# Key chunks of the loop as three products of rounded parts, with the context split on GpSimd

## The reference, cut to what matters

```python
q = (layernorm(x) @ w_q.T)         # x: 8 batches, 56 queries, 128 wide; 16 heads of 8
k = (ctx @ w_k.T)                  # ctx: 8 batches, 1500 keys, 128 wide
v = (ctx @ w_v.T)
attn = softmax(q k^T * HEAD_DIM ** -0.5)
x = x + tanh(g_xattn) * (attn v @ w_o.T)
x = x + tanh(g_ffn) * experts(layernorm(x))   # 8 experts, top 2, GELU, F = 512
```

## Time and profile before

| what | value |
|---|---|
| median of 3 runs | 293.86 us (292.49 to 294.77) |
| the profiled execution | 293.01 us, its span 291.3 us |
| granted TensorE clock, mean of the span | 0.994 |
| attention loop with its tail | about 27 to 211 us of the span |

### The profile page before, as it was taken

The page is one execution under the profiler, slowest core; times in us unless marked ns, Lnnn a source line. Parts: engine busy times, 40 slices in busy tenths (PEclk is TensorE's granted clock), DMA queues, the critical chain, the costliest instruction groups (busy, mean ns, idle before and its releaser), DMA issues.

```text
span 291.3 us, 8035 instructions
## 1 busy us (share of the span) xinstructions
PE 279.3 (96%) x2826; PEld 223.8 (77%) x2826; DVE 217.8 (75%) x420; ACT 178.7 (61%) x370; POOL 103.0 (35%) x113
## 2 busy tenths in 40 slices
PE   7988999999999999999999999999899999998994
PEld 2464888878878887887888898987688888887862
DVE  5688878768787687787876877877155988888861
ACT  2635586766766767568568674567517776665500
POOL 4598632052043033224206201024501466676300
PEclk9999799999999999999999999999999999999999
DMA  7397932970991892693397299200000000000001
GB/s 256 96 202 196 223 97 60 263 212 12 248 223 53 214 233 83 164 243 123 96 248 185 52 214 279 101 0 2 2 2 0 1 0 0 0 1 0 2 0 32
DMA packets 9924, 32.19 MB, mean 111 GB/s; under 512 B 2576, under 2 KB 3088, under 8 KB 9904
## 3 DMA queue, kind: packets, MB, share of 16 engines
q1 hardware_dynamic: 9472, 31.60, 42.4%
q10 hardware_dynamic: 432, 0.33, 0.3%
HBM read 13.26 MB, written 0.23 MB: 46 GB/s over the span
## 4 chain that ended last, share of the span: by engine, by line
PE 86%; DVE 5%; ACT 3%; DMA 2%; issue 1%; POOL 1%; SPq 0%; DVEq 0%; ACTq 0%
PE max_ps L963 16%; PE score_ps L943 15%; PE o_ps L977 14%; PE misc_ps L931 8%; PE misc_ps L925 5%; PE score_ps L1185 4%; PE score_ps L1186 3%; PE score_ps L1187 3%; PE o_ps L1267 2%; PE o_ps L1185 1%; ACT probs L514 1%; PE o_ps L1187 1%; PE o_ps L1186 1%; PE max_ps L993 1%; PE misc_ps L1098 1%
## 5 line engine op out<-in xcount | busy, mean ns | idle before, releaser
L700 DVE TENSOR_REDUCE part_max<-max_ps 112x1 f32<-112x512 f32 (+1 forms) x192 | 116.2, 669 | 35.1 <-PE max_ps L963 34.4
L514 ACT ACTIVATE probs<-score_ps 128x448 f32<-128x448 f32 x192 | 90.2, 555 | 13.5 <-PE score_ps L943 12.1
L963 PE MATMUL max_ps<-kx,qx 96*112 96x512 f32 (+1 forms) x192 | 81.1, 428 | 2.0 <-DVE part_max L700 0.9
L943 PE MATMUL score_ps<-qx,kx 104*128 104x224 f32 (+1 forms) x384 | 76.6, 285 | 0.6 <-ACT probs L514 0.4
L943 PEld LDWEIGHTS score_ps<-qx,kx 104*128 104x128 f32 (+1 forms) x384 | 67.0, 190 | 11.2 <-issue 3.2
L977 PE MATMUL o_ps<-probs,v_sb 128*32 128x112 f32 (+1 forms) x1536 | 43.9, 261 | 1.1 <-ACT probs L514 1.1
L977 PEld LDWEIGHTS o_ps<-probs,v_sb 128*32 128x32 f32 (+1 forms) x1536 | 35.7, 110 | 9.1 <-ACT probs L514 6.1
L963 PEld LDWEIGHTS max_ps<-kx,qx 96*112 96x112 f32 x192 | 34.2, 179 | 7.1 <-issue 2.9
L366 POOL TENSOR_TENSOR k_low<-k_full,k_high 128x512 fp32r<-128x512 f32 (+1 forms) x21 | 26.3, 1252 | 33.2 <-ACT k_full L497 32.9
L399 POOL TENSOR_TENSOR o_norm<-o_sb,inv_den 128x112 f32 (+1 forms) x15 | 6.3, 422 | 81.3 <-DVE inv_den L726 81.3
L509 ACT ACTIVATE v_sb<-misc_ps 128x512 f32<-128x512 f32 x24 | 14.4, 600 | 31.2 <-PE misc_ps L931 31.2
(11 more groups left out here) (177 smaller groups left out, 376.2 us busy)
## 6 DMA issues: line engine op xcount, KB each, us to landing
kx<-k_high SPq DMA_DIRECT2D x60, 187.5 KB, 5.1
kx<-k_low SPq DMA_DIRECT2D x30, 187.5 KB, 4.9
ctx_sb<-in_ctxT SPq DMA_DIRECT2D x7, 750.0 KB, 5.8
gu_sb<-in_guT SPq DMA_DIRECT2D x8, 512.0 KB, 5.3
dn_sb<-in_dnT SPq DMA_DIRECT2D x8, 256.0 KB, 5.4
ctx_sb<-in_ctxT SPq DMA_DIRECT2D x2, 256.0 KB, 4.2
kx<-k_high SPq DMA_DIRECT2D x4, 123.5 KB, 2.3
kx<-k_high SPq DMA_DIRECT2D x4, 64.0 KB, 2.0
```

What stands on the lines that cost most here:

```text
L514: nc.scalar.activation(probs[:, (KT * h + t) % 8, :], score_ps[:, t % 3, 0:SC // 2], ACT.Exp, scale=SCALE).then_inc(exp_done, 1)
L700: nc.vector.reduce_max(part_max[:, p, c:c + 1], max_ps[0:PC, bank, 0:size], AX.X).then_inc(max_taken, turns)
L943: last = nc.tensor.matmul(score_ps[0:m, t % 3, GC * g:GC * g + GC], kx[0:KR, 2 * par + h, g, 128 * t:128 * t + m], qx[0:KR, par, 2 * h + g ...
L963: nc.tensor.matmul(max_ps[0:PC, bank, 0:size], qx[0:MR, par, 2 * h + p // 2, PC * (p % 2):PC * (p % 2) + PC], kx[0:MR, slot, p // 2, start ...
```

## The change

The 18 key chunks of the loop are made by three fp32r matmuls (high part of the weights by high part of the context, high by low, low by high) instead of one fp32 matmul. The weights' parts are made once by POOL ahead of the loop. The context's parts are made by POOL for each chunk (`split_context`: an addition of a broadcast zero that writes the rounded part, then a subtraction), into two buffers used in turn, and PE waits for them on `ctx_split`. Two of the first batch's splits stand ahead of `ones_rows(2)`, the third in the first body. SP loads a batch's context in three chunks with a semaphore each. The keys of odd batches take the room of experts 5 to 7 in `gu_sb`, so that these three experts are loaded only after the last odd keys have been moved; POOL's, ACT's and PE's wait for them (`late_loaded`) stands later, in the FFN. POOL's loop has two turns and its last two bodies are written out.

```diff
         def _(sp):
+            def load_chunk(b, par, n):
+                start, size = chunk(n)
+                sp.dma_start(ctx_sb[:, par, start:start + size], ctxT[b][:, start:start + size]).then_inc(chunk_loaded[par][n], 16)
...
                 if ctx_next:
+                    sp.wait_ge(v_done, NCH * (b + 1) + 2)
+                    load_chunk(b + 3, 1 - par, 0)
+                    load_chunk(b + 3, 1 - par, 1)
                     sp.wait_ge(v_done, NCH * (b + 2))
-                    sp.dma_start(ctx_sb[:, 1 - par, 0:TK], ctxT[b + 3]).then_inc(ctx_loaded[1 - par], 16)
+                    load_chunk(b + 3, 1 - par, 2)
...
             pool.wait_ge(consts, 1)
+            nc.gpsimd.memset(no_shift[:, :], 0.0).then_inc(wk_split, 1)
+            pool.wait_ge(wk_split, 1)
+            pool.wait_ge(wk_loaded, 16)
+            nc.gpsimd.tensor_copy(wk_parts[:, 0, :], wk_sb[:, :]).then_inc(wk_split, 1)
+            pool.wait_ge(wk_split, 2)
+            nc.gpsimd.tensor_tensor(wk_parts[:, 1, :], wk_sb[:, :], wk_parts[:, 0, :].bitcast(f32), ALU.subtract
+                                    ).then_inc(wk_split, 1)
+            pool.wait_ge(wk_split, 3)
...
+            def split_context(i, par, n):
+                start, size = chunk(n)
+                side, made = (par + n) % 2, NCH * batch(i, par) + n + 1
+                src = ctx_sb[:, par, start:start + size]
+                pool.wait_ge(chunk_loaded[par][n], 16 * (i + 1))
+                nc.gpsimd.tensor_tensor(ctx_parts[:, side, 0, 0:size], src, bc(no_shift[:, :], [128, size]), ALU.add
+                                        ).then_inc(ctx_high, 1)
+                pool.wait_ge(ctx_high, made)
+                nc.gpsimd.tensor_tensor(ctx_parts[:, side, 1, 0:size], src, ctx_parts[:, side, 0, 0:size].bitcast(f32),
+                                        ALU.subtract).then_inc(ctx_split, 1)
+
             pool.wait_ge(k_low_saved, 2 * NCH)
+            split_context(0, 0, 0)
+            pool.wait_ge(ctx_split, 1)
+            pool.wait_ge(nm_step, 6)
+            split_context(0, 0, 1)
+            pool.wait_ge(ctx_split, 2)
             ones_rows(2)
             ones_rows(3)
...
                 stage(b + 2, par, 0)
+                pool.wait_ge(qx_ready, 2 * b + 5)
+                pool.wait_ge(k_done, NCH * (b + 2) + 1)
+                split_context(i, par, 2)
+                pool.wait_ge(ctx_split, NCH * (b + 1))
                 k_rest(b + 2, par, 1)
                 k_rest(b + 2, par, 2)
                 normalise(i, par, 0)
+                if more:
+                    pool.wait_ge(o_norm_ready, FIRST_NORM + 2 * b + 1)
+                    pool.wait_ge(k_done, NCH * (b + 2) + 2)
+                    split_context(i1, par1, 0)
+                    pool.wait_ge(ctx_split, NCH * (b + 1) + 1)
+                    pool.wait_ge(k_done, NCH * (b + 3))
+                    pool.wait_ge(scores_done, KT * (2 * b + 2) + 1)
+                    split_context(i1, par1, 1)
+                    pool.wait_ge(ctx_split, NCH * (b + 1) + 2)
                 normalise(i, par, 1)
...
+            def k_product(i, par, n):
+                size = chunk(n)[1]
+                pe.wait_ge(ctx_split, NCH * batch(i, par) + n + 1)
+                for k, (w, c) in enumerate(((0, 0), (0, 1), (1, 0))):
+                    last = nc.tensor.matmul(misc_ps[:, 0:size], wk_parts[:, w, :], ctx_parts[:, (par + n) % 2, c, 0:size],
+                                            start=(k == 0), stop=(k == 2), skip_group_check=True)
+                last.then_inc(k_done, 1)
...
                 if h == 0 and c == 0:
-                    pe.wait_ge(ctx_loaded[par], 16 * (i + 2))
                     pe.wait_ge(v_saved, NCH * (b + 1) + 1)
-                    k_project(b + 2, par, 0, misc_ps)
+                    k_product(i, par, 0)
```

More of the change, by code:

```diff
@@ L183, in flamingo_block @@
         k_done, k_saved, k_low_saved = map(sem, ("k_done", "k_saved", "k_low_saved"))
+        wk_split, ctx_high, ctx_split, late_loaded = map(sem, ("wk_split", "ctx_high", "ctx_split", "late_loaded"))
+        chunk_loaded = [[sem(f"chunk_loaded{par}{n}") for n in range(NCH)] for par in range(2)]
         v_done, v_saved = map(sem, ("v_done", "v_saved"))
@@ L245, in move_keys @@
                 eng.dma_start(kx[32 * row:32 * row + 32, 2 * par + h, g, start:start + size].bitcast(f32),
-                              src[r:r + 32, par, start:start + size].bitcast(f32)).then_inc(landed, 16)
+                              src[par][r:r + 32, start:start + size].bitcast(f32)).then_inc(landed, 16)
         @block.sync
         def _(sp):
+            def load_chunk(b, par, n):
+                start, size = chunk(n)
+                sp.dma_start(ctx_sb[:, par, start:start + size], ctxT[b][:, start:start + size]).then_inc(chunk_loaded[par][n], 16)
             def move_unit(par, h):
@@ L270, in _ @@
             sp.wait_ge(v_done, NCH)
-            sp.dma_start(ctx_sb[:, 0, 0:TK], ctxT[2]).then_inc(ctx_loaded[0], 16)
+            for n in range(NCH):
+                load_chunk(2, 0, n)
             sp.wait_ge(k_low_saved, 2 * NCH)
@@ L286, in body, with load_expert @@
                 move_unit(par, 1)
[L287 to L292, removed]
+                if early:
+                    load_expert(b)
+            def load_expert(e, loaded=ffn_loaded):
+                sp.dma_start(gu_sb[:, e, :], guT[:, e, :]).then_inc(loaded, 16)
+                sp.dma_start(dn_sb[:, e, :, :], dnT[:, e, :, :]).then_inc(loaded, 16)
             with sp.Fori(0, 2) as i:
@@ L297, in _ @@
             body(2, 0)
-            body(2, 1, ctx_next=False)
-            for e in range(B - 2, E):
-                load_expert(e)
+            body(2, 1, ctx_next=False, early=False)
+            for h in range(2):
+                for g in range(2):
+                    sp.wait_ge(kx_loaded[2 + h][g], MOVES * B // 2)
+            for e in range(LATE, E):
+                load_expert(e, late_loaded)
             sp.wait_ge(out_ready, NR)
@@ L402, in normalise, with body @@
                                         ).then_inc(o_norm_ready, 1)
-            def body(i, par):
+            def body(i, par, more=True):
                 b = batch(i, par)
+                i1, par1 = nxt(i, par, 1)
                 pool.wait_ge(scores_done, KT * 2 * b + 1)
@@ L413, in body @@
                 normalise(i, par, 0)
+                if more:
[7 more added lines that the diff above has]
+                    pool.wait_ge(ctx_split, NCH * (b + 1) + 2)
                 normalise(i, par, 1)
-            with pool.Fori(0, B // 2 - 1) as i:
+            with pool.Fori(0, 2) as i:
                 body(i, 0)
                 body(i, 1)
+            body(2, 0)
+            body(2, 1, more=False)
             pool.wait_ge(scores_done, KT * (NU - 4) + 1)
@@ L493, in k_copy @@
                 act.wait_ge(k_done, NCH * b + n + 1)
-                nc.scalar.activation(k_high[:, par, start:start + size], bank[:, 0:size], ACT.Copy
+                nc.scalar.activation(k_high[par][:, start:start + size], bank[:, 0:size], ACT.Copy
                                      ).then_inc(k_saved, 1 if whole else 2)
@@ L690, in k_rest @@
                 dve.wait_ge(k_saved, 2 * (NCH * b + n + 1))
-                nc.vector.tensor_tensor(k_low[:, 0, start:start + size], bank[:, 0:size],
-                                        k_high[:, 0, start:start + size].bitcast(f32), ALU.subtract
+                nc.vector.tensor_tensor(k_low[0][:, start:start + size], bank[:, 0:size],
+                                        k_high[0][:, start:start + size].bitcast(f32), ALU.subtract
                                         ).then_inc(k_low_saved, 1)
```

35 lines of the change are left out of this document (22 added, 13 removed).

## The result

| what | before | after |
|---|---|---|
| median, the runs of that measurement | 293.26 us (6 runs) | 296.35 us (295.77 to 297.48, 6 runs) |
| ratio | | 1.0094, 95% interval 1.0056 to 1.0132 |
| profiled execution, its span | 293.01 us, 291.3 us | 297.39 us, 295.6 us |
| granted clock, mean of the span | 0.994 | 0.982 |
| POOL busy | 103.0 us | 145.0 us |

A forecast was written before the change was run, and what follows sets the result against it. PE was taken to bound the loop from end to end. From 293.0 us, 2.5 saved, 3.7 of standing and 1.7 of clock gave 295.9 us profiled, 296.8 us median with 0.85 us added; range 292.6 to 298.8 us.

The forecast's parts named there:

- The stand: First loop body: PE idles 3.7 us from 44.30 us until POOL's third split ends at 48.0; bounds 2.9 to 4.1.
- The rival in which POOL is in time: First body: POOL finishes the third split by 44.0 us, so PE never stands; 291.1 us, chance 0.10.
- The Trainium skill's rule: POOL's splits: two-input operations cost about 2.6 cycles an element, so broadcast saves nothing; PE's idle time 0.3 us longer.
- The clock: PE's clock falls to half rate again around the first body's idle stretch, costing 1.7 us; bounds nothing and 2.5 us.
- The products: Loop's 18 key chunks: three fp32r matmuls save 0.16 us for each of 12, 0.145 for each of 6; 2.8 us.
- a saving of 0.16 us fits into both: Steady loop: PE came 0.35 us behind DVE and 0.39 us behind ACT, so the chunk saving would be kept.
- one of my own signs of being wrong: Steady loop: the prediction is wrong if PE's waits for DVE and ACT at L986 and L977 grow in every unit.
- The rival of a third gone: Loop: DVE and ACT take one third of the saving, beside PE's idle stretch; +1 us, 297.8 us, chance 0.10.
- The 0.08 us that I gave to the change of format: Ahead of a fp32 chunk, the last fp32r matmul takes 0.30 us instead of 0.22; expected to remain behind the product.
- The steady loop: Later bodies: POOL's three splits add 7.1 us per 23.5 us body, all covered by gaps; cost nothing.
- The weights' parts: Ahead of POOL's `q_parts` work: three small POOL instructions may overlap DVE's first block-diagonal operation; 0 to 0.4 us, taken as nothing.
- The sum: Whole kernel: 293.0 - 2.5 + 3.7 + 1.7 = 295.9 us profiled, 296.8 us for the median, 1.0% slower.

The follow-up runs named there:

- The filled stand: Changed kernel with PE's first loop turn written out and 16 unread matmuls of 128 columns ahead of the third chunk's wait: 294.56 us, ratio 1.0040 to the kernel before.
- the control: Changed kernel with only the first turn of PE's loop written out: 297.05 us, ratio 1.0126 to the kernel before.
- fp32 chunks in the same order: Changed kernel with both `ones_rows` memsets ahead of POOL's `nm_step` wait, loop key chunks by one fp32 matmul, POOL's splits kept: 293.21 us, ratio 0.9948.
- free cast, held clock: Changed kernel with `ones_rows(2)` ahead of the `nm_step` wait, `ones_rows(3)` behind the first `normalise`, eight unread matmuls ahead of the loop: 289.75 us, ratio 0.9867.
- the kernel before with the extra matmuls: Kernel before the change with only eight unread matmuls of 128 columns added ahead of the loop: 291.83 us, ratio 0.9941.
- the kernel with one memset moved: Changed kernel with only `ones_rows(2)` moved ahead of POOL's wait for `nm_step`: 292.64 us, ratio 0.9948 to the kernel before.

## Why the prediction came out right

**The stand** is the step that carried it. I had POOL's queue from 34.2 to 48.0 us and a stand of 3.7 us from PE's old time, 4.0 with PE's earlier arrival. Measured: 48.13 and 3.93 us. Each term was near: the additions took 1.04 and 0.98 us (1.06 and 0.99 taken from `stage`), the memsets 5.37, the gap 0.39. The rival in which POOL is in time falls.

The Trainium skill's rule that I set against it (GPSIMD Engine Reference, section 3.1, a `tensor_tensor` of two inputs at about 2.6 cycles an element) would have had the addition at the subtraction's 1.28 us; with a broadcast second input it took 1.04 us. Here the measurement decides against the rule for this form. (By my own bounds the rule would have made the stand 0.4 us longer, not the 0.3 us that stand there.)

**The clock** was put at 1.7 us, between 0 and 2.5. The filled stand says 1.6 us against the changed kernel by the ratios; the profiled execution lost 2.1 us. The 2.5 us to the control hold some of the first fall too. Right in kind, and near in size.

**The products** were mis-sized. I took 2.8 us with 1.8 us as the low end, and let 2.5 us stay. Three measurements say 1.7 us (medians, fp32 chunks in the same order), 1.6 us (18 times the trace's 0.09 us) and 2.1 us (free cast, held clock, the change as a whole). The product's own 0.70 and 0.65 us were right; the step that failed is "a saving of 0.16 us fits into both" gaps behind it. In PE's loop 0.24 us pass from DVE's end to PE's start even when PE waits (0.12 us in the turn written out), so of 0.27 to 0.36 us only 0.03 to 0.12 were free. Half of one of my own signs of being wrong did show: the wait for DVE at L986 grew in every unit of the steady loop, by 0.05 to 0.12 us. The rival of a third gone had the true size. The gap to ACT ahead of `attend` did hold. The 0.08 us that I gave to the change of format are something else, for the last product of the maxima starts 0.31 us ahead of the fp32r chunk too (84.87 to 85.18); what they are stays open. The longer first tile at a turn of the loop was not foreseen and stays unexplained; writing out one turn gained nothing that can be seen.

**The steady loop** at nothing was right: fp32 chunks with all of POOL's new work stay at the kernel before's time. POOL was 42 us busier and not 46; my own 2.4 and 2.3 us a split would have said 43. **The weights' parts** cost nothing either: DVE's operation there, 0.61 us, was not held up.

**The sum** was closer than its terms, and that is luck. Both errors push the same way: a smaller saving and a dearer clock each make the kernel slower than forecast. With the measured terms, 3.9 us for the stand, 1.6 to 2.1 for the clock and 1.7 to 2.1 saved, it should be 3.4 to 4.3 us slower. The profiled execution is, with 4.3 us. The forecast was 2.9 us, and the six runs give 2.8 us, with an interval of 1.6 to 3.9 us and the median between three runs that lost less to the clock and three that lost more.

## What to carry to other kernels

Where a change hangs the busiest engine on another, walk the other's queue through the first turn of the loop as well as a steady one: the work from ahead of the loop lies there, and one wait put in front of it moves all of it. Ask next what the clock does with the new gap: here it added about half of the stand's own time. And a saving is only as large as the slack to the next engine less the time that the hand-over takes, and that time has to be read from a place where the engine really waits; here it was twice as long in PE's loop as in the turn written out.

## What the hardware showed

- A DVE cast of 112 partitions by 4 columns is held up by POOL's memset until that ends: 0.17 us became 0.60, 0.61, 1.59 and 1.60 us in four profiles. POOL's `stage` does it as well: in the kernel before with the extra matmuls the cast took 0.45 us and ended at 33.33, POOL's operation at 33.30. DVE's reductions beside it, the tensor_reduce of 12 columns in SBUF among them (0.17 us), were not touched. The Trainium skill (SBUF — State Buffer, its section on the two separate sides) calls this an exclusive lock of a shared port pair, held for the whole instruction; the trace agrees, with the 1.59 us above. The page says it of DVE operations in a two-port mode; whether the cast ran in one, no trace here shows.
- A split does it to DVE's subtraction of 112 by 4 as well. Inside the stand of the changed kernel it took 0.96 us instead of 0.16 and ended at 46.88, POOL's addition at 46.86. It cost nothing there, since PE stood anyway, and happened nowhere else in that profile.
- From the end of DVE's subtraction to the start of PE's `transpose_max` at least 0.23 us passed in PE's loop, even where PE had stood 1.3 us for it (0.24 us). With the turn written out it was 0.12 to 0.19 us, and at the `transpose_max` behind the loop 0.06 us (203.29 to 203.35). So 0.24 us is no least time of the two engines.
- The clock stayed low for 6.8 us (45.8 to 52.6) though PE worked again after 2.4 of them. The first fall lasted 3.4 us in the profile of the kernel before, and 7 us in that of the kernel with one memset moved. The mean clock of one kernel differs by execution, from 0.982 to 0.993.
- The same small gaps ahead of the loop bring a fall of the clock, at 28.4 to 30.2 us in the profiles that have it, and not in every execution: one profile of two of the same kernel had none. With extra matmuls of 128 columns, two behind each of four maxima, the clock stayed at 2.4 GHz there in the profiles of all three kernels that had them.
